# Three-bank rings, one TensorE increment per step, and edge attributes read back from DRAM, in a three-layer graph network

## The reference

```python
def layers(x, src, dst, edge_type, edge_attr, weights, roots, biases, edge_w, edge_b):
    # x: 6250 x 256; 100000 edges, sorted by dst; 3 edge types; edge_attr: 100000 x 32
    ew = edge_attr @ edge_w + edge_b                       # 100000 x 256
    masks = [(edge_type == i) for i in range(3)]
    inv_cnt = [1.0 / max(segment_sum(m, dst), 1.0) for m in masks]
    for l in range(3):
        msg = relu(x[src] * ew)
        out = 0
        for i in range(3):
            h = segment_sum(msg * masks[i], dst) * inv_cnt[i]
            out = out + h @ weights[l, i]
        x = x + relu(out + x @ roots[l] + biases[l])
    return x

result = layernorm(x + layers(x, ...))
```

## Time and profile before

| | us |
|---|---|
| median of 3 runs | 2967.97 |
| lowest, highest | 2964.79, 2969.89 |
| span of the profiled execution | 3581.6 |

### The profile page before, as it was taken

One profiled execution on the slowest core, in us unless ns is written; L12 is line 12 of the kernel. 1 busy time (PEld: TensorE's weight loads), 2 busy tenths in 40 slices (PEclk: granted clock), 3 DMA queues, 4 the chain that ended last, 5 costly groups with the idle time before them and its releaser, 6 DMA issues.

```text
span 3581.6 us, 59909 instructions
## 1 busy us (share of the span) xinstructions
PE 2843.8 (79%) x18436; PEld 2613.2 (73%) x18436; DVE 2148.4 (60%) x6028; ACT 1289.4 (36%) x2738; POOL 2224.3 (62%) x2364
## 2 busy tenths in 40 slices
PE   6888888888888877787777877777777777787777
PEld 6777777777777777777777777767777777776776
DVE  5666666666666555555555555555556656665665
ACT  5555555555555322222222222222222222222222
POOL 6666666666666566666666666656666666666664
PEclk9999999999999888888898889988888888899898
DMA  6554555555455444444444444444444444444443
GB/s 148 135 137 132 137 135 138 136 137 137 131 137 145 133 120 127 125 130 127 126 127 127 134 124 127 131 127 132 126 124 128 125 127 131 125 130 124 128 128 99
DMA packets 334989, 465.42 MB, mean 130 GB/s; under 512 B 158995, under 2 KB 221646, under 8 KB 334670
## 3 DMA queue, kind: packets, MB, share of 16 engines
q0 software_dynamic: 112608, 307.65, 30.1%
q1 hardware_dynamic: 221244, 153.70, 15.6%
q10 hardware_dynamic: 818, 0.18, 0.0%
HBM read 403.94 MB, written 57.36 MB: 129 GB/s over the span
## 4 chain that ended last, share of the span: by engine, by line
PE 59%; issue 17%; DVE 9%; another core or an unknown queue 8%; ACT 4%; DVEq 2%; DMA 0%; ACTq 0%
PE bank L911 29%; PE bank L867 14%; PE bank L961 12%; DVE acc L1138 4%; PE bank L846 2%; DVE xg L1300 1%; ACT oh_a L812 1%; DVE t L1155 1%; ACT at L753 1%; DVEq L1274 1%; PE bank L936 1%; DVEq L1138 1%; ACT xg L791 1%; DVE S L1097 1%
## 5 line engine op out<-in xcount | busy, mean ns | idle before, releaser
L700 POOL DMA_INDIRECT xg<-x,idx x1540 | 1457.0, 946 | 870.6 <-issue 351.7
L911 PE MATMUL bank<-S,xg 128*128 128x96 f32 x9384 | 1450.5, 304 | 360.3 <-issue 176.3
L911 PEld LDWEIGHTS bank<-S,xg 128*128 128x128 f32 x9384 | 1313.6, 216 | 429.2 <-issue 385.4
L791 ACT ACTIVATE xg<-xg 128x512 f32<-128x512 f32 x1170 | 736.7, 630 | 2102.3 <-DVE xg L1300 1193.8
L1300 DVE TENSOR_TENSOR xg<-xg,bank 128x512 f32<-128x512 f32 x1170 | 800.8, 684 | 691.0 <-remote 329.4
L1138 DVE TENSOR_TENSOR acc<-acc,bank 128x192 f32 x2346 | 816.7, 348 | 570.0 <-PE bank L911 343.0
L867 PE MATMUL bank<-wsb,at 128*128 128x256 f32 x4692 | 985.7, 337 | 213.6 <-issue 123.3
L700 POOL DMA_INDIRECT xg<-in_x_dram,idx x782 | 742.2, 949 | 454.2 <-PE bank L911 211.2
L867 PEld LDWEIGHTS bank<-wsb,at 128*128 128x128 f32 x4692 | 749.3, 214 | 297.6 <-issue 195.9
L961 PE MATMUL bank<-W,acc 128*128 128x256 f32 (+1 forms) x1764 | 515.9, 415 | 7.2 <-issue 6.4
L961 PEld LDWEIGHTS bank<-W,acc 128*128 128x128 f32 (+1 forms) x1764 | 386.9, 258 | 17.3 <-issue 12.1
(11 more groups left out here) (75 smaller groups left out, 789.7 us busy)
## 6 DMA issues: line engine op xcount, KB each, us to landing
at<-attr_t SPq DMA_DIRECT2D x390, 128.0 KB
attr_t<-at SPq DMA_DIRECT2D x195, 128.0 KB
xg<-x,idx POOLq DMA_INDIRECT x1540
xg<-in_x_dram,idx POOLq DMA_INDIRECT x782
hs<-in_edge_attr_dram SPq DMA_DIRECT2D x194, 64.0 KB
x<-t SPq DMA_DIRECT2D x96, 128.0 KB
xblk<-x SPq DMA_DIRECT2D x96, 128.0 KB
y<-t SPq DMA_DIRECT2D x94, 128.0 KB
```

Source lines behind the costliest of these rows:

```text
L700: eng.indirect_dma_start(out=xg[:, n % XR, :], out_offset=None, in_=rows_in, in_offset=bass.IndirectOffsetOnAxis(ap=rows_at, axis=0)).then ...
L791: eng.activation(v, v, ACT.Relu).then_inc(s_r, 1)
L911: last = eng.matmul(sums_bank(l, q, i)[:, 192 * i + 96 * h:192 * i + 96 * h + 96], xg[:, n % XR, 128 * h:128 * h + 128], S[:, slot(l, 2 * ...
```

## The change

- Attributes are transposed on the host: `attr_q` holds, for each group of four tiles, 128 rows of 128 numbers (32 features x 4 tiles, 128 edges). `load_attr` reads them, `high` and `split` work on that form, and `keep_attr` writes both parts to `attr_t` straight from `hs`. `attr_turn` and `attr_copy` are gone. `reload_attr` fills `at` in layer 0 too.
- Edge weights, transposed x and the last block's first products share a ring of three banks `pE` (0, 1, 4); sums use a ring of three, `pA` (2, 3, 5). Edge weights are formed two steps ahead instead of one, and sums are added three steps later instead of two. The row of numbers that `S` is compared with, which was in bank 5, is now in each bank of `pA`.
- TensorE increments `s_sc` once a step; waits for edge weights, transposed x and mixed products go by it as well. `collect` comes after `mix` and `turn_x` in a step.
- Counts of a block are copied to `kept` by VectorE before TensorE sums them.

```diff
-        pE = bank[0:2]
-        pA = bank[2:4]
+        pE = [bank[0], bank[1], bank[4]]
+        pA = [bank[2], bank[3], bank[5]]
...
+        def high_step(g):
+            return -6 if g == 1 else -5 if g == 2 else max(2 * g - 8, g - 3)
+        def split_step(g):
+            return high_step(g) + 1
+        def keep_step(g):
+            return max(split_step(g), -4)
+        def load_step(g):
+            return max(2 * g - 11, g - 6)
+        def reload_step(g):
+            return max(2 * g - 5, keep_step(g) + 1)
...
+        def collected(l, q):
+            return l * (NP + 1) + q + 1 + (q == NP - 1)
+        def wait_edges(eng, l, q):
+            if q < 3:
+                eng.wait_ge(s_e, 3 * l + q + 1)
+            else:
+                eng.wait_ge(s_sc, collected(l, q - 3))
...
             def keep_attr(g):
-                w = 128 * tiles_of(g)
-                eng.wait_ge(s_atc, g + 1)
-                eng.dma_start(attr_t[g, :, 0:w], at[0:64, g % TR, 0:w].bitcast(F32)).then_inc(s_ao[g % TR], 16)
+                eng.wait_ge(s_lo, g + 1)
+                eng.dma_start(attr_t[g].rearrange("(h f) (i e) -> (f i) h e", h=2, i=4),
+                              hs[:, g % 3, :, :]).then_inc(s_ao[g % 3], 16)
...
             def reload_attr(l, g):
                 G = l * NG + g
-                eng.wait_ge(s_e, l * NP + 2 * max(0, g - TR + 1))
+                if l == 0:
+                    eng.wait_ge(s_ao[g % 3], 16 * (g // 3 + 1))
+                if g >= TR:
+                    wait_edges(eng, l, 2 * (g - TR) + 1)
+                elif l:
+                    wait_edges(eng, l - 1, NP - 1)
...
-            def attr_turn(g):
-                eng.wait_ge(s_lo, g + 1)
-                eng.wait_ge(s_atc, g)
-                eng.wait_ge(s_xc, turned[0])
-                for i in range(tiles_of(g)):
-                    last = eng.transpose(pT[0:64, 128 * i:128 * i + 128], hs[:, g % 3, i, :], ident[:, :])
-                last.then_inc(s_tr, 1)
...
-                    last.then_inc(s_sc, 1)
+                    if i or q == NP - 1:
+                        last.then_inc(s_sc, 1)
...
-                        if (1 if l else 0) <= q < NP - 1:
-                            edge_weights(l, q + 1)
+                        if (0 if l else -1) <= q < NP - 2:
+                            edge_weights(l, q + 2)
...
                         if q == NP - 1:
+                            add_sums(l, q - 3, 0)
                             selectors(l, q)
+                            if l == 0:
+                                add_counts(q - 3)
+                            add_sums(l, q - 3, 1)
                             add_sums(l, q - 2, 0)
...
-                        if 0 <= q - 2 < NP:
-                            add_sums(l, q - 2, 0)
+                        if 0 <= q - 3 < NP:
+                            add_sums(l, q - 3, 0)
```

More of the change, by code:

```diff
@@ L247, in tile @@
             return head_tile(order[n // 4]) + n % 4
-        short = order.index(quad(NT - 1))
-        def attrs(g):
-            return 16 * (g // 3 + 1) + (16 if g % 3 == short % 3 and g >= short else 0)
+        def high_step(g):
[8 more added lines that the diff above has]
+            return max(2 * g - 5, keep_step(g) + 1)
         def starting(q, lag):
@@ L290, in twice, with shared_bank, free_shared_bank, products @@
             return sum(n % NB < NB - 1 for n in range(i, min(K, NB * (L - 1)), TB))
+        end = starts[-1] + 18
+        users = [("edges", 0, 0)]
+        for l in range(L):
+            for q in range(-3, end):
+                if (0 if l else -1) <= q < NP - 2:
+                    users.append(("edges", l, q + 2))
+                if l < L - 1 and q == NP + 1:
+                    users.append(("edges", l + 1, 0))
+                if l < L - 1 and q == end - 1:
+                    users.append(("edges", l + 1, 1))
+                if q == mix_step(l, NB - 1, 0):
+                    users.append(("last", l, NB - 1))
+                users += [("turned", l, k) for k in range(NB) if q == turn_step(k)]
+        turn_of = {u: i for i, u in enumerate(users)}
+        def shared_bank(what, l, i):
+            return pE[turn_of[what, l, i] % 3]
+        def free_shared_bank(eng, what, l, i):
+            before = turn_of[what, l, i] - 3
+            if before < 0:
+                return
+            what, l, i = users[before]
+            if what == "edges":
+                eng.wait_ge(s_m, l * NP + i + 1)
+            elif what == "turned":
+                eng.wait_ge(s_xc, NB * l + i + 1)
+            else:
+                eng.wait_ge(s_f0, NB * l + i + 1)
+        def products(l, k, m):
+            last = shared_bank("last", l, NB - 1)
+            b = pD[m // 2] if k < NB - 1 else (last, last, pD[0], pD[1])[m]
+            return b[0:rows(k), 256 * (m % 2):256 * (m % 2) + 256]
         hosts = [16, 12]
@@ L309, in slot @@
             return 4 * ((l * NQ + j // 4) % (SR // 4)) + j % 4
-        end = starts[-1] + 16
         heads = 12
@@ L628, in fast @@
                         if l < L - 1 and q == NP:
-                            for i in range(0 if l else TR):
-                                eng.wait_ge(s_ao[i], 16 * uses(1, i, TR, NG))
                             for g in range(TR):
@@ L981, in fast @@
                                 count(k)
+                        for k in range(NB):
+                            for m in range(R + 1):
+                                if q == mix_step(l, k, m):
+                                    mix(l, k, m)
+                        for k in range(NB):
+                            if q == turn_step(k):
+                                turn_x(l, k)
                         if 0 <= q - 1 < NP:
@@ L1016, in _ @@
             eng.wait_ge(s_cst, 4)
-            link(eng.tensor_copy(steps_of, iota[:, :]))
+            for q in range(3):
+                link(eng.tensor_copy(steps_of(0, q, 0, WK + 1), iota[:, 0:WK + 1]))
             split(0)
@@ L1240, in block_ops @@
                 if wide(l, k):
-                    return [o for f in ops for o in (f, pause)]
+                    return [first, mean0, pause, mean1, mean2, residual]
                 return ops if l < L - 1 else ops + [add_x, stats, aggr, pause, recip, shift]
@@ L1330, in fast @@
                             break
-                        if 0 <= q - 2 < NP:
-                            add_sums(l, q - 2, 0)
+                        if 0 <= q - 3 < NP:
+                            add_sums(l, q - 3, 0)
                         if 0 <= q < NP and q % 2 == 0:
                             selectors(l, q)
-                        if l == 0 and q % 2 and 1 <= (q + 6) // 2 < NG:
-                            split((q + 6) // 2)
+                        if l == 0:
+                            for g in [g for g in range(1, NG) if q == split_step(g)]:
+                                split(g)
                         for k in list(todo):
@@ L1341, in fast @@
                         for k in range(NB):
[L1342 removed]
+                            if q == starts[k] + 3 and k < NB - 1:
                                 todo[k] = block_ops(l, k)
                         if l == 0:
[L1345 removed]
+                            if 0 <= q - 3 < NP:
+                                add_counts(q - 3)
+                            for k in starting(q, 0):
+                                if k < NB - 1:
+                                    keep_counts(k)
+                            for i, lag in ((0, 3), (1, 4)):
                                 for k in starting(q, lag):
```

269 lines of the change are left out of this document (131 added, 138 removed).

## The result

The changed kernel takes 2983.77 us (median of 4 runs, 2981.09 to 2988.63), the kernel before 2966.38 us beside it (4 runs, 2963.86 to 2969.89). The ratio is 1.0061, 95% interval 1.0049 to 1.0073: slower by 17.4 us. The prediction said 2972.5 within 2953 to 2984, and 0.46 for no change that can be measured against 0.35 for slower. The changed kernel's profiled execution took 2988.63 us, with a span of 2986.9.

A forecast was written before the change was run, and what follows sets the result against it. The prediction took GpSimd's gather launches, 1.25 us apart, to bound the kernel. To the median of 2968 us it added 3 for the start and 1.5 for the layer ends, other terms 0: 2972.5, range 2953 to 2984.

The forecast's parts named there:

- The bound: Whole kernel: runs go at the pace of GpSimd's gather launches, one per 1.25 us, nearly from end to end.
- Rival 2: Whole kernel: TensorE sets the runs, so losing layer 0's transposes saves 131 us, time about 2837; chance 0.06.
- Layer 0's work: Layer 0's TensorE and ScalarE: transposes and PSUM copies that go are covered by the launches; cost and gain 0.
- One increment: TensorE's semaphore increments each step: two fewer could be 62 us if on the path; taken as 0.
- Three banks: Edge products and sums on TensorE: running a step further ahead delays nothing late; 0 to -11 us, taken as 0.
- The start: Kernel start: first attribute groups wait for a bare store and reload, delaying step 0's sums; +3 us taken.
- Reloads of layer 0: Attribute reloads throughout layer 0: they fit the time in hand, 2.2 us spare at the worst end; cost 0.
- Layer ends: Three layer ends: VectorE has one more pair of adds ahead of its last multiplication; 0 to +2.7 us, taken +1.5.
- Joint stops: Profiled execution: VectorE, ScalarE and TensorE stand still together for 2.9 to 3.0 us; taken as recording, absent from runs.
- Rival 3: Layer changes: last block and next layer's first sums wait for more adds, one 2.5 us step each; 2980, chance 0.15.

The follow-up runs named there:

- e5: The kernel before, unchanged, run again for a trace without joint stops: 2966.56 us (10 runs).
- e6: The changed kernel, unchanged, as a control on the chip without stops: 2985.67 us (5 runs), ratio 1.0064 to the kernel before.
- e7: The kernel before with the attribute path alone changed, on the chip without stops: 2975.03 us (6 runs) against 2966.30, ratio 1.0028.
- e8: Changed kernel; groups 0 to 2 straight from host, adds caught up at layer ends, group 3's reload before block loads, zero rows in one piece: 2980.87 us.
- f3: The changed kernel with as many semaphore increments as before given back, on a semaphore nobody waits for: 2985.15 us (4 runs).
- f4: The kernel before with one increment of the sums' semaphore a step instead of one a tile: 2966.02 us (11 runs), ratio 1.0000.
- f1: The changed kernel with two idle TensorE products a step added in each layer's last nine steps and the one after: 2982.60 us, ratio 1.0055.
- e4: The kernel before with the attribute path alone changed, on a chip with stops: 3582.26 us against 3580.75, ratio 1.0004.

## Why the prediction was wrong

- *The bound: right.* Launches stay 1.25 us apart at the median in e5, e6, e7 and e8, and removing the transposes, 131 us of TensorE's work by the earlier trace rows, gained nothing. Rival 2 is refuted.
- *Layer 0's work, 0: right.* Layer 0 from its 13th launch to its last takes 965.5 us with the transposes and 965.3 without (e5, e7).
- *One increment, 0: right* (f3, f4). The estimate of 62 us from the Trainium skill, TensorE: Matmul & The Clock Gate, The cost: per-tile semaphore tail, does not appear: as many increments given back changed the time by -0.5 us, less than these runs tell apart. That fits a TensorE that is off the path for most of the time.
- *Three banks, "0 to -11, I take 0": wrong, and the step that failed.* It measured some +11 us (19.4 less the 8.7 of e7). The step says that the new order delays "nothing that is late"; I read that off one place, the last step of a trace with stops, and carried it over to the layer changes. There TensorE's list does stand on the path. Two things were found there. One is the granted clock: 501 instead of 225 us of the span are at the low level, and 2.90 us became 4.53 for one group alone, with the sums ahead of it 2.00 for 1.11; f1, f3 and f4 put the level's worth at 2 to 5 us at the first layer change and 2 to 3 at the end. The low level was in the rows of the start, and I gave it no thought elsewhere. The other is the late reload below. Why three banks come with the lower clock, and where the rest of the 11 comes from, stays open. A bound of "no gain" was no bound on a loss.
- *The start, +3 of 1.5 to 7.4: the mechanism was right, the term low.* It measured +4.2 (e7) to +4.4 (e6). The two pieces of the sum hold: reloads bare behind the flag, and the sums of step 0 behind the second one, at 25.38 within the 24.2 to 28.0 reckoned. Part of the difference is what it was counted from: the thirteenth launch of the trace with stops, at 22.46, against which 25.65 is +3.2; in e5 it starts at 21.13. By the Trainium skill, DMA: Bandwidth & Descriptors, Anatomy of one DMA — SWDGE (gpsimd) path, a transfer has about 2.0 us fixed, so the pair takes at least 4.0 us, an estimate. The section is on GpSimd's transfers and these are SyncE's; the trace agrees with it as a lower bound, with 21.39 - 15.47 = 5.9 us from the store's issue to the products behind the reload.
- *Reloads of layer 0, 0: right in the one execution of e7 that was traced.* But transfers cost at two places that the sum did not have: 2.5 us after the zero rows, and the reload of group 3 at layer 2's start, which stands behind six block loads (5.3 us in that section of the table, 4.9 of them back in e8). Both transfers and their places in the queue were in the kernel before as well, and TensorE waited 2.52 us for that reload in e5 and 4.34 in e6; what tipped them over was not isolated.
- *Layer ends, +1.5 from one more pair of adds: the size of the whole was +14.* The clock and the late reload are the parts of it that were found. Moving the adds (e8) left the first layer change at 22.2, under the low clock; what they cost under the high one, where 1 to 2 us remain (f3, f1 against e5), was not tested.
- *Joint stops are "part of recording; the runs have no room for them": wrong as a general claim.* The runs first shown have none. Runs on three other chips have them, at 3542 to 3594 us.
- *Rival 3, 2980 by the refill: the nearest time, by the wrong mechanism.* It blamed adds and a step lost at three places; what was found there is the clock and a late reload. So the nearness is luck.

## What to carry to other kernels

When one engine sets the pace, look for the places where its work stops being ahead: the start, the changes between layers, the end. There another engine's list stands on the path, and there its granted clock counts. The version with three banks had the lower clock here (0.927 against 0.9575 with the attribute path alone), for a reason that stays open; so read the clock at those places before costing a change of TensorE's list at nothing. One trace can mislead: the level at a layer's end differed between executions of nearly the same kernel, so read several before crediting a repair. A repaired wait at the head of a queue may only hand the wait to the next transfer in it, so read the next one first.

## What the runs showed of the hardware

The same kernel has its stops on some chips and not on others. e4's groups, on a chip with stops, against e5's above (the two kernels take the same time on such a chip):

```profile
L715 POOL DMA_INDIRECT xg<-x,idx x1540 | 1459.9, 948 | 864.9 <-issue 358.5 <-PE bank L901 273.3 <-remote 233.1
L715 POOL DMA_INDIRECT xg<-in_x_dram,idx x782 | 741.8, 949 | 454.0 <-issue 179.2 <-PE bank L901 177.4 <-remote 95.8
```

A launch takes as long; the idle time nearly doubles, in stops about 6.1 us apart in layer 0 and 9.0 in the others, where 115 to 140 recorded instructions lie between two. The traces with stops hold 18,000 to 21,000 updates of semaphores, those without some 70,000. All timed runs on those chips have the long time too. Whether recording causes the stops is not settled, since no run here was without it.

At the low level of TensorE's clock the last block's twelve passes took 4.53 us, at the high level 2.90. With 1.06 us of idle products a step (f1) the level was high at all three layer ends and the first layer change 3.8 us shorter than in e6; f3 had the high level at two of them without those products, so this is no proof of a remedy. And two stores of 128 pieces of 8 bytes were followed by a gather for which VectorE waited 5.4 us, in the kernel before 2.9; stored as one piece each (e8, with three other repairs), no wait there was over 1.1.
